# Gathering the even source one-hots of two adjacency sums from an identity matrix in memory

## The reference

```
h = relu(layernorm(x))
# layer 0, attention over edges
e     = relu(concat(h[src], h[dst]) @ W_kind + b_kind)     # kind hh, oo or ho, by edge number
logit = e @ W_a + b_a
alpha = softmax of logit over the edges of one dst
z     = segment_sum(alpha * h[src], dst)
x     = x + relu(concat(h, z) @ W_node + b_node)           # W_hn or W_on by node
# layer 1, weighted graph convolution
h     = relu(layernorm(x))
c     = edge_weight / sqrt(w_out[src] * w_in[dst])
agg   = deg_in^-1/2 * segment_sum(c * deg_out^-1/2 * h[src], dst)
x     = x + relu(agg @ W + b)
```

## Time and profile before

| | |
|---|---|
| median of 3 runs | 698.67 us (698.03 to 701.55) |
| the profiled execution | 698.53 us |
| its span, first to last instruction | 696.7 us |
| mean granted TensorE clock | 0.911 of full speed |
| first adjacency, TensorE | 391.4 to 473.7 us of the span |
| second adjacency, TensorE | 488.4 to 545.4 us of the span |

### The profile page before, as it was taken

The page is one execution under the profiler, slowest core; times in us unless marked ns, Lnnn a source line. Parts: engine busy times, 40 slices in busy tenths (PEclk is TensorE's granted clock), DMA queues, the critical chain, the costliest instruction groups (busy, mean ns, idle before and its releaser), DMA issues.

```text
span 696.7 us, 9145 instructions
## 1 busy us (share of the span) xinstructions
PE 560.0 (80%) x2844; PEld 416.5 (60%) x2844; DVE 518.7 (74%) x824; ACT 287.2 (41%) x338; POOL 222.1 (32%) x178
## 2 busy tenths in 40 slices
PE   0999897997987069754996487868989699999996
PEld 0887786786876058533874243426444487877785
DVE  6754355499879969987796999988998537687224
ACT  3512347563201002312433699963788227314210
POOL 1300000377655713733233344004799000121000
PEclk9999899998998669957998699986999899999999
DMA  8982622899999999897758378003100064503002
GB/s 307 345 348 92 241 92 90 328 402 409 411 416 409 410 316 331 317 368 271 262 197 338 107 221 245 5 32 97 56 1 1 1 242 150 188 25 122 1 30 91
DMA packets 43658, 144.85 MB, mean 208 GB/s; under 512 B 5409, under 2 KB 5729, under 8 KB 43617
## 3 DMA queue, kind: packets, MB, share of 16 engines
q1 hardware_dynamic: 22496, 69.85, 27.9%
q0 software_dynamic: 18432, 67.12, 25.5%
q10 hardware_dynamic: 2688, 7.37, 3.1%
HBM read 131.70 MB, written 12.62 MB: 207 GB/s over the span
## 4 chain that ended last, share of the span: by engine, by line
PE 42%; DVE 31%; issue 11%; POOL 6%; DMA 5%; DVEq 3%; ACT 1%; SPq 1%; ACTq 0%; POOLq 0%
PE banks L942 23%; DVE rows L651 7%; PE banks L1033 6%; POOL rows L385 5%; DVE masked L673 4%; PE banks L1084 4%; DVE w_lo L595 4%; DMA rows<-table,ids_i 4%; PE banks L1101 4%; DVE pick_dst L764 4%; PE banks L989 3%; DVE rows L652 2%; DVEq L761 2%; DVE fT_lo L839 2%; PE banks L1045 1%
## 5 line engine op out<-in xcount | busy, mean ns | idle before, releaser
L385 POOL DMA_INDIRECT rows<-table,ids_i x124 | 148.6, 1199 | 249.7 <-DVE rows L652 123.9
L942 PE MATMUL banks<-w_hi,fT_hi 128*128 128x512 f32 x392 | 160.8, 410 | 56.5 <-DVE stage L685 28.1
L433 ACT ACTIVATE w_hi<-w_raw 128x1024 fp32r<-128x1024 f32 x88 | 92.2, 1060 | 271.6 <-PE banks L942 150.2
L595 DVE TENSOR_TENSOR w_lo<-w_raw,w_hi 128x1024 fp32r<-128x1024 f32 x88 | 106.5, 1223 | 95.9 <-ACT w_hi L433 95.4
L942 PE MATMUL banks<-w_lo,fT_hi 128*128 128x512 f32 x392 | 158.7, 405 | 0.0
L942 PE MATMUL banks<-w_hi,fT_lo 128*128 128x512 f32 x392 | 158.1, 403 | 0.0
L942 PEld LDWEIGHTS banks<-w_hi,fT_hi 128*128 128x128 f32 x392 | 77.4, 197 | 78.2 <-issue 29.4
L1033 PE MATMUL banks<-pick_src,pick_dst 128*128 128x512 bf16 x420 | 108.0, 397 | 8.4 <-issue 3.6
L942 PEld LDWEIGHTS banks<-w_hi,fT_lo 128*128 128x128 f32 x392 | 77.3, 197 | 16.8
L942 PEld LDWEIGHTS banks<-w_lo,fT_hi 128*128 128x128 f32 x392 | 77.5, 198 | 16.0
L651 DVE TENSOR_TENSOR rows<-rows 128x1024 f32<-128x1024 f32 x62 | 75.7, 1222 | 13.6 <-DMA rows<-table,ids_i 13.2
(11 more groups left out here) (149 smaller groups left out, 626.9 us busy)
## 6 DMA issues: line engine op xcount, KB each, us to landing
w_raw<-in_L_gnn_W_ho_dram SPq DMA_DIRECT2D x16, 512.0 KB
table<-stage SPq DMA_DIRECT2D x32, 256.0 KB, 4.7
w_raw<-in_L_gnn_W_oo_dram SPq DMA_DIRECT2D x16, 512.0 KB
w_raw<-in_L_gnn_W_on_dram SPq DMA_DIRECT2D x16, 512.0 KB
w_raw<-in_L_gnn_W_hn_dram SPq DMA_DIRECT2D x16, 512.0 KB
w_raw<-in_L_gnn_W_hh_dram SPq DMA_DIRECT2D x16, 512.0 KB
w_raw<-in_L_gnn_W_dram SPq DMA_DIRECT2D x8, 512.0 KB
dst_rep<-in_dst_dram ACTq DMA_DIRECT2D x6, 512.0 KB, 10.6
```

Source lines behind the costliest of these rows:

```text
L385: pool.indirect_dma_start(out=rows[:, slot, side, :], out_offset=None, in_=table[kind][side], in_offset=bass.IndirectOffsetOnAxis(ap=ids_i ...
L433: act.activation(w_hi[:, c % 4, :], w_raw[:, c % SLOTS, :], ACT.Copy).then_inc(hi_done, 1)
L595: dve.tensor_tensor(w_lo[:, c % 4, :], w_raw[:, c % SLOTS, :], w_hi[:, c % 4, :].bitcast(F32), ALU.subtract).then_inc(lo_done, 1)
L942: ins = pe.matmul(bank[j][:, :], fT[a][:, k, m * P:(m + 1) * P], wS[b][:, slot, n * H:(n + 1) * H], start=(k == 0 and p == 0), stop=(k == ...
```

## The change

The even source one-hots are no longer computed. VectorE makes a 512 x 512 identity matrix once near the start (four `tensor_scalar` in bf16, laid over buffer space that the row slots use later). ScalarE's queue stores it to memory (`eye_row`, 512 KB) after weight chunk 5. For every pair, in both adjacencies, GpSimd issues one indirect DMA which gathers 128 rows of 1 KB of it, by the source numbers of the even tile, straight into `pick_src[...][:, 0, :]`. In the first adjacency these gathers stand between GpSimd's row fetches: four ahead of fetch 53, then two behind each fetch from 53 to 60, and the last twelve behind fetch 61. ScalarE makes only the odd half in both adjacencies. TensorE waits for the gather's semaphore in place of `even_ready`, and now in the first adjacency too.

```diff
+        eye, _ = sb("eye", [P, B, N], BF16, over=at + REPS * CE * 4)
+        eye_row = nc.dram_tensor("eye_row", [N, N], BF16, kind="Internal").ap()
...
+            def fetch_one_hot(pair, first_pair):
+                slot = pair % RING
+                if first_pair + pair >= RING:
+                    pool.wait_ge(adj_done, first_pair + pair - (RING - 1))
+                pool.indirect_dma_start(out=pick_src[slot][:, 0, :], out_offset=None, in_=eye_row,
+                                        in_offset=bass.IndirectOffsetOnAxis(ap=ids_i[:, 0, 2 * pair:2 * pair + 1], axis=0)
+                                        ).then_inc(src_in[slot], 16)
...
+            pool.wait_ge(eye_out, 16)
             for i in range(TE):
...
+                if i == MIX + ROWS:
+                    pool.wait_ge(hh_logits, TILE_HH)
+                    for pair in range(RING):
+                        fetch_one_hot(pair, 0)
                 fetch(i)
+                if i >= MIX + ROWS:
+                    first = 2 * (i - MIX - ROWS) + RING
+                    for pair in range(first, first + 2 if i < TE - 1 else T // 2):
+                        fetch_one_hot(pair, 0)
             power(1, f_dst, wsum, wsum_ready, fac_ready)
             power(1, f_src, w_out, wdeg_ready, fac_ready)
             for pair in range(T // 2):
-                pool.wait_ge(adj_done, T // 2 + pair - (RING - 1))
-                t = 2 * pair
-                pool.tensor_scalar(pick_src[pair % RING][:, 0, :], node_no[:, :], ids_f[:, 0, t:t + 1], None,
-                                   ALU.is_equal).then_inc(even_ready, 1)
+                fetch_one_hot(pair, T // 2)
...
+                if c == 5:
+                    act.wait_ge(eye_made, 1)
+                    act.dma_start(eye_row.rearrange("(b p) n -> p b n", p=P), eye[:, :, :]).then_inc(eye_out, 16)
...
-                pick(pair, (0, 1), 0)
+                pick(pair, (1,), 0)
...
+            for b in range(B):
+                ins = dve.tensor_scalar(eye[:, b, :], node_no[:, :], node_id[:, b:b + 1], None, ALU.is_equal)
+            ins.then_inc(eye_made, 1)
...
-                    if not deg:
-                        pe.wait_ge(even_ready, pair + 1)
+                    pe.wait_ge(src_in[slot], 16 * ((first_pair + pair) // RING + 1))
```

More of the change, by code:

```diff
@@ L206, in build @@
         lift_ready = sem("lift_ready"); lift_out = sem("lift_out"); lift_in = sem("lift_in"); max_done = sem("max_done")
-        pair_ready = sem("pair_ready"); odd_ready = sem("odd_ready"); even_ready = sem("even_ready"); own_act = sem("act_step"); adj_done = sem("adj_done"); adj_full = sem("adj_full")
+        pair_ready = sem("pair_ready"); odd_ready = sem("odd_ready"); eye_made = sem("eye_made"); eye_out = sem("eye_out"); src_in = [sem(f"src_in{r}") for r in range(RING)]; own_act = sem("act_step"); adj_done = sem("adj_done"); adj_full = sem("adj_full")
         adj_ready = sem("adj_ready"); adjT_done = sem("adjT_done"); adjwT_ready = sem("adjwT_ready")
```

## The result

The changed kernel is slower: 705.33 us (median of 4 runs, 702.89 to 709.37) against 698.35 us, ratio 1.011 with a 95% interval of 1.0073 to 1.0147. A second set of runs gave 707.35 us against 698.33 us, 1.0141 (1.0102 to 1.018). The first profiled execution spans 701.8 us against 696.7.

A forecast was written before the change was run, and what follows sets the result against it. The prediction took VectorE to bound the first adjacency and TensorE's own pace the second. From the profiled 698.5 us, 0 and -1.0 gave 697.5, with 0.1 for the median 697.6; 8-in-10 range 694 to 706.

The forecast's parts named there:

- Net **0: First adjacency: VectorE's added waits of +1.9 us and its saved waits of -2.1 us cancel, so no change.
- the gathers of pairs 0 to 3: Start of second adjacency: the first four gathers replace four comparisons under the softmax chain and cost 0.
- Rival 2: First adjacency: GpSimd becomes the bound, +5.8 us at 1.378 us a gather, total 701 to 706; chance 0.20.
- ScalarE's part and the identity matrix, 0: ScalarE's saved passes in the first adjacency and making the identity near the start, both hidden: 0.
- The pace of GpSimd: First adjacency, fetches 53 to 60: four gathers a tile cost GpSimd 6.1 us against VectorE's 4.83.
- Sum **+1.9 us: First adjacency's end: VectorE waits +1.2 us before spread 24 and +0.7 before spread 25 for late pairs.
- fetch 54 starts at about 398.0: First adjacency: pair 5's gather waits for pair 1, closed at 396.3, so fetch 54 starts later than 395.05.
- The landing, 2.3 us: Gathered one-hots, both adjacencies: 2.3 us from issue to landing; a landing of 4.6 would add +2.3 in the first.
- The waits of 0.50 and 1.64 us go: -2.1 us: First adjacency's end: VectorE's waits for TensorE at pairs 30 and 31 vanish, saving 2.1 us.
- The second adjacency, -1.0: Second adjacency: faster `pick_dst` gives -1.5 us through TensorE's waits, a lost lead +0.5; net -1.0 us.
- lead of the instruction stream: Second adjacency, pairs 1 to 5: they ran at 1.32 us from this lead; gathers arriving just in time lose it, +0.5.
- Rivals 1 and 3: Second adjacency: gather latency paces it, 702 to 707, chance 0.17; or producers had paced TensorE, 691, chance 0.11.

The follow-up runs named there:

- one-side run: Changed kernel with one-hot gathers in the first adjacency only, and no destination-side rows fetched for tiles 53 to 61: 0.9972 of the kernel before.
- small rows: Changed kernel with one-hot gathers in the first adjacency only, and row fetches 53 to 61 of 1 KB rows, not 4 KB: 1.005 of the kernel before.
- experiment 6: Changed kernel with one-hot gathers in the second adjacency only, each pair's gather held until the pair before it is closed: 839.31 us.

## Why the prediction was wrong

The measured time of 705.33 us lies just inside the range of 694 to 706, the second set's 707.35 us outside it. I forecast a wash at 0.52, and the kernel is slower by 1.1 to 1.4%. Two terms that I put at 0 failed: the first adjacency's "Net **0**" measured +6.5 us, and the gathers of pairs 0 to 3 of the second one, also 0, measured +3.8. Rival 2 with its chance of 0.20 is nearest to what happened, but its range of 701 to 706 us was hit in part by luck: it asked for gathers of 1.378 us, and they took 1.13, and 3.8 us of the loss lie in a stretch that no rival named.

1. **ScalarE's part and the identity matrix, 0: right.** Making it took VectorE 1.27 us for all four, and the products' unbroken piece on TensorE is still 43.82 us. The first adjacency of the one-side run, with ScalarE's full relief, took the 82.9 us of before.
2. **The pace of GpSimd: right, 6.26 us a tile for my 6.1, 5.97 of it its own work.** It came from the right row; a gather in that loop took 1.13 us for my 1.2. "With gathers of 0.95 us ... GpSimd keeps up" was wrong in itself: 4 x 1.28 is 5.1 us, above 4.83. The failed step is what I made of the pace: that VectorE waits 1.2 us at spread 24 and 0.7 at spread 25, the "Sum **+1.9 us**". The waits stand at spreads 11, 17 and 21 and are 7.4 us. I followed the lateness only for pairs 20 and 21 at the end of the loop, with pairs at 1.78 us each; but pair 7 takes two rounds, TensorE ran pair 6 at a granted clock of 0.50 behind its pause of 4.3 us (2.72 us for six matmuls), and so the lead was gone by spread 11. Above all I took the time from a closed pair to its announcement as nothing. It was up to 3.7 us, and by the estimate above it makes 6.1 of the 7.4.
3. **"fetch 54 starts at about 398.0"**, 7.5 us behind fetch 53: it was 9.7. I had named the wait but taken pair 1's end from the trace before, where it closed 5.0 us behind the first matmul; in the changed profile that was 6.0, which makes 0.8 us counted from fetch 53. The rest is that pair 5's gather started 1.7 us behind this closing, where pair 4's started 0.5 us behind its own. Why is open. That fetch 61 then started at 441.15 us, where I had 440.7, is luck: this profile's first adjacency began 3.1 us earlier than the one I had counted from.
4. **The landing, 2.3 us: right where I had put it, in an empty queue (2.28), and too small behind the rows (3.9).** No row of the kernel before shows the 2.3: it was an estimate between the 2.0 us of a store and the 4.6 of a fetch. I had 4.6 as the bound and priced it at +2.3; with small rows the length of the one profile fell by 0.3, the runs' ratio by 0.4% with overlapping intervals.
5. **"The waits of 0.50 and 1.64 us go: -2.1 us": wrong in size, -0.8.** I had counted on TensorE to reach pair 26 sooner and to run it faster than before, but `chunk_max(6)` and `edge(61)` lie between for VectorE: TensorE had closed pair 25 4.6 us before pair 26 was announced, and the six matmuls of pair 26 took 2.72 us at a granted clock of 0.50, as in the kernel before. No run shows the -2.1: the changed profile left 0.50 and 0.88, the second one 0.53 and 0.42, which is -1.2.
6. **The second adjacency, -1.0: right, -0.8 in the mean of two profiles.** `pick_dst` fell to 612 ns and the ring held: pairs stay 1.6 us apart. The "lead of the instruction stream" behind the +0.5 is shown by no run; from the first closing to the seventh it took 8.0 and 8.3 us in the two profiles before, 9.2 and 8.3 after. Rivals 1 and 3 both failed.
7. **"The gathers of pairs 0 to 3 stand where four comparisons stood ... 0": wrong, +3.8.** I costed their engine time and not what they might do to others. They lie beside the product with `member`, whose `me_done` is on the chain there, and it was announced 2.95 us behind its last matmul. This term was in no rival.

What stays open is why an announcement of TensorE comes late. For the product with `member`, four indirect gathers issued over its end brought the lateness in all three profiles; one that ends ahead of it does not do it, nor do four plain DMAs of the same size, nor SyncE's 512 KB; and the announcement follows the last issue by about 1 us. In the first adjacency the same lateness is read from the traces of the kernels that gather there, and not tested by a run of its own; in the changed profile the announcements of pairs 7 and 13 also came 1.0 to 1.1 us behind the end of an issue, that of pair 17 came 0.6 us behind one. That TensorE goes on with pair 14 while three engines wait for pair 13 speaks for its semaphore and against its instructions as what is held. How much of the loss would be left with GpSimd at 6 us a tile but every announcement in time was not tried, nor was a ring deeper than four, or a pause in GpSimd's queue between the gathers.

## What to carry to other kernels

When work is moved to an engine that feeds a loop, compare its cost per round of the loop with the round of the engine that sets the pace, and if it is above, follow the lateness through every round with all waits of its queue (here fetch 54 came 9.7 us behind fetch 53, where it had been 4.5); a buffer's lead delays the loss only until it is used up, here by pair 11 of 32. Where a wait is longer than expected, compare its end with the end of the instruction that was waited for, and with the other engines that wait for the same semaphore: that tells late work from a late announcement. What the gathers saved on ScalarE was worth nothing here (its load from 390 to 432 us fell from 36.78 to 18.55 us, and the first adjacency of the one-side run took the 82.9 us of before), and the gathers' issue is work too: three per round were free (beside a pacing engine at 4.83 us a round), four cost 5 to 7 us. Look at what else is on the chain at the moment at which a new transfer is issued, not only at whether its own engine is free.

## What the runs showed of the hardware

- A GpSimd indirect DMA of 128 rows of 1 KB took 0.94 us at the least to issue, 0.97 in the mean of the second adjacency and 1.10 in the first, with 0.30 us between two that followed without a wait (changed kernel). In the loop of the first adjacency, the 18 row fetches of 1 KB rows took 1.18 us in the mean (small rows) and the 18 of 4 KB rows 1.19 (changed kernel), so the size of a row did not set the cost there.
- It was usable by TensorE 2.28 us behind the end of its issue in an empty queue (experiment 6), 1.9 to 4.0 us behind it with 1 KB row gathers ahead (small rows, six waits), 3.5 to 4.4 us with 4 KB ones (changed kernel, five waits; 3.0 to 4.7 at the seven of its second profile).
- Four indirect gathers issued across the end of a run of 256 small matmuls delayed the announcement of that run: the length between the adjacencies was 17.5 to 18.4 us in three profiles, where it was 14.1 in the kernel before. With 512 KB from SyncE there it was 13.9, with four plain DMAs from GpSimd 14.5.
- In the first adjacency with four indirect gathers a tile, some of TensorE's increments of `adj_done` reached ScalarE, GpSimd and VectorE 0.9 to 4.1 us behind the closing matmul (profile of the changed kernel), where in the kernel before it was 0.04 us (ScalarE, all waits of that stretch) and 0.40 us (VectorE, at both of its waits).
- VectorE's two-input `pick_dst` took 732 ns beside GpSimd's comparison and 612 ns beside GpSimd's gathers (changed kernel).
- Six matmuls of a pair took 1.46 us at a granted clock of 1.00 and 2.72 us at 0.50 (pairs 6 and 26 of the changed kernel, behind pauses of TensorE of 4.3 and 4.6 us, and the pairs of experiment 6).
